# Four column tiles for the projections and the transposes of maxima in a decoder kernel on one core

## The chip, the cores and the metric

The kernel runs on one core of one Trainium2 chip. The metric is the device time of one launch in microseconds. TensorE (PE) multiplies, VectorE (DVE) and ScalarE (ACT) work on vectors, GpSimdE (POOL) helps them, SyncE (SP) issues the transfers. Each engine runs its own list of instructions in order, and they wait for each other by semaphores.

## The reference

32 sequences of 256 tokens with 256 features go through one decoder layer:

```python
x = x + attn(layernorm(x))            # 16 heads of 16, rotary positions, 256 keys
x = x + xattn(layernorm(x), ctx)      # 16 heads of 16, 77 keys
x = x + ffn(layernorm(x))
# ffn: 6 nodes, each an attention with 8 heads of 32 over earlier nodes
for c in range(6):
    nsrc = min(c + 1, 5); s = c - nsrc
    q = ew[c, 0] * (nodes[c - 1] @ We[eq] + be[eq])
    k = ew[c, 1] * (nodes[s] @ We[ek] + be[ek])
    v = ew[c, 2] * (nodes[s + nsrc // 2] @ We[ev] + be[ev])
    nodes[c] = act_w[c] * mha(q, k, v, Wq[c], Wk[c], Wv[c], Wo[c]) + q
out = layernorm(nodes[5])             # with gain and shift
```

All inputs and outputs are float32.

## The kernel before

A preamble multiplies the edge weights of the nodes with the heads' weights, so that each node needs one projection each for q, k and v, and puts all weights into SBUF. Then a loop runs 16 turns. A turn takes two sequences, slot 0 and slot 1, through eight stages: 0 is self attention, 1 cross attention, 2 to 7 the nodes. The two slots stand at different stages, so that one has work for PE while the other waits.

The work is cut into 838 pieces a turn. The text ORDER lists them, written out by hand or by a planner, and each engine runs its own pieces in that order. A word is a kind, the slot, the stage and, for some, a group of heads and a part. "@5" gives the PSUM bank (S and ST take four banks from it), and a "+" marks a piece that belongs to the next pair of sequences and is run once ahead of the loop. The last turn leaves those out.

PE's pieces are:
- TR transposes the normed tokens. Q and QB, K, V make the projections, QR and KR rotate q and k for the positions with a 128x128 matrix.
- S and SB make scores with the queries on the partitions, from which VectorE takes row maxima (MX, L879). Both factors are split into a high and a low fp32r part. These matmuls have 32 rows, one group of heads each, and four of them stand side by side in four row tiles.
- GpSimdE splits the negated maxima into two parts (NM, L695 and L698), MT transposes them (L1028), ScalarE copies them to SBUF (MR, L780).
- ST makes the scores again with the keys on the partitions, SX adds the negated maxima to them by a matmul with a selector, and ScalarE takes exp from there (EX, L789).
- PV multiplies the exponentials with ones (the sums) and with the values. Each of these matmuls writes 32 partitions, and four of them stand side by side in four column tiles.
- After RC and NR have divided by the sums, OA and OB make the output of a stage: XA adds it to the residual stream, or NE keeps it as the next node.

LOADX and LOADC load tokens and contexts, STORE writes a result, all from SP's queue. LNS, LNP, LNN norm.

Before the change Q, QB, K, V, QR, KR, OA and OB use all 128 columns of the array, for V of the cross stage 77. They go through the helper matmul, so that all of them have line L909, as have S, SB, ST, SX and PV; in the trace they are told apart by the tiles that they read. MT uses PE's transpose, 128x128, two for a piece.

Of the kernel before, what the change touches and what calls it, by code (L numbers as in the profile page):

```python
# [139 lines left out]
NM0.1.0 PV1.0.1 NM0.1.1 MT0.1.0@5 ST1.0.3@0 SX1.0.3 RC1.0.0 MR0.1.0 PV1.0.2@7 MT0.1.1@5 EX1.0.3.0 EX1.0.3.1  # L140
ST0.1.0@0 SX0.1.0 EX0.1.0.0 MR0.1.1 PV1.0.3 EX0.1.0.1 ST0.1.1@0 SX0.1.1 NR1.0.0 PV0.1.0@4 OB1.0.0@6 RC1.0.1
NR1.0.1 EX0.1.1.0 EX0.1.1.1 OB1.0.1 ST0.1.2@0 SX0.1.2 EX0.1.2.0 EX0.1.2.1 V1.1@7 VE1.1 PV0.1.1 RC0.1.0 XA1.0
LNS1.1 LNP1.1 LNN1.1 +LOADX0 +LNS0.0 PV0.1.2@5 ST0.1.3@0 SX0.1.3 EX0.1.3.0 EX0.1.3.1 NR0.1.0 +LNP0.0 +LOADC0
TR1.1@6 +K0.1@7 TRE1.1 PV0.1.3 Q1.1@1 QB1.1 RC0.1.1 NR0.1.1 QH1.1.0 QH1.1.1 QL1.1.1 QL1.1.0 +KI0.1 OB0.1.0@4
OB0.1.1 XA0.1 S1.1.0@0 SB1.1.0 MX1.1.0.0 MX1.1.0.1 S1.1.1@4 SB1.1.1 MX1.1.1.0 S1.1.2@0 SB1.1.2 MX1.1.1.1 NM1.1.1
NM1.1.0 MX1.1.2.0 MX1.1.2.1 S1.1.3@4 SB1.1.3 MX1.1.3.0 MT1.1.0@1 MR1.1.0 ST1.1.0@0 SX1.1.0 MX1.1.3.1 NM1.1.2
NM1.1.3 MT1.1.1@6 EX1.1.0.1 MR1.1.1 LNS0.2 LNP0.2 XB1.1 LNN0.2 ST1.1.1@4 SX1.1.1 EX1.1.0.0 PV1.1.0@1 TR0.2@2
EX1.1.1.0 EX1.1.1.1 ST1.1.2@4 SX1.1.2 TRE0.2 Q0.2@0 QB0.2 EX1.1.2.0 EX1.1.2.1 PV1.1.1 QH0.2.0 QH0.2.1 QL0.2.0
+LNN0.0 ST1.1.3@4 SX1.1.3 RC1.1.0 NR1.1.0 QL0.2.1 K0.2@3 PV1.1.2@2 EX1.1.3.1 EX1.1.3.0 PV1.1.3 +KH0.1 KH0.2
KL0.2 RC1.1.1 S0.2.0@4 SB0.2.0 +LOADC1 +KL0.1 +K1.1@3 +KI1.1 NR1.1.1 OB1.1.0@0 OB1.1.1 V0.2@2 K0.3@3 KH0.3  # L150
MX0.2.0.1 XA1.1 LNS1.2 LNP1.2 MX0.2.0.0 LNN1.2 S0.2.1@4 TR1.2@0 TRE1.2 NM0.2.0 MT0.2.0@1 SB0.2.1 KL0.3 K1.2@3
MR0.2.0 KH1.2 VE0.2 Q1.2@1 QB1.2 QH1.2.0 QH1.2.1 MX0.2.1.1 MX0.2.1.0 NM0.2.1 QL1.2.1 KL1.2 QL1.2.0 ST0.2.0@4
SX0.2.0 EX0.2.0.0 EX0.2.0.1 K1.3@2 KH1.3 KL1.3 MT0.2.1@0 MR0.2.1 S1.2.0@4 SB1.2.0 MX1.2.0.1 MX1.2.0.0 NM1.2.0
PV0.2.0@1 RC0.2.0 V1.2@2 VE1.2 ST0.2.1@4 SX0.2.1 EX0.2.1.0 EX0.2.1.1 NR0.2.0 K0.4@1 KH0.4 MT1.2.0@2 MR1.2.0
S1.2.1@4 SB1.2.1 MX1.2.1.1 MX1.2.1.0 PV0.2.1@3 RC0.2.1 OA0.2@0 ST1.2.0@4 SX1.2.0 EX1.2.0.1 EX1.2.0.0 KL0.4
NM1.2.1 MT1.2.1@1 MR1.2.1 OB0.2.0 NR0.2.1 OB0.2.1 NE0.2.0 NE0.2.1 ST1.2.1@4 SX1.2.1 EX1.2.1.1 EX1.2.1.0 Q0.3@1
QB0.3 PV1.2.0@0 QH0.3.0 QH0.3.1 QL0.3.0 QL0.3.1 S0.3.0@4 SB0.3.0 MX0.3.0.1 MX0.3.0.0 NM0.3.0 RC1.2.0 NR1.2.0
PV1.2.1@1 OA1.2@3 S0.3.1@4 SB0.3.1 OB1.2.0 MT0.3.0@2 K1.4@0 RC1.2.1 NR1.2.1 MX0.3.1.0 OB1.2.1 MX0.3.1.1
ST0.3.0@4 MR0.3.0 SX0.3.0 NE1.2.0 +KH1.1 Q1.3@1 NE1.2.1 QB1.3 V1.3@2 KH1.4 KL1.4 NM0.3.1 EX0.3.0.1 EX0.3.0.0
MT0.3.1@6 QH1.3.0 QH1.3.1 QL1.3.1 QL1.3.0 V0.3@3 MR0.3.1 S1.3.0@4 SB1.3.0 VE0.3 VE1.3 PV0.3.0@2 MX1.3.0.1  # L160
MX1.3.0.0 ST0.3.1@4 SX0.3.1 RC0.3.0 NR0.3.0 OA0.3@3 NM1.3.0 MT1.3.0@1 EX0.3.1.0 EX0.3.1.1 S1.3.1@4 SB1.3.1
MX1.3.1.0 MX1.3.1.1 PV0.3.1@0 MR1.3.0 RC0.3.1 OB0.3.0 NM1.3.1 MT1.3.1@2 MR1.3.1 ST1.3.0@4 SX1.3.0 EX1.3.0.0
EX1.3.0.1 NR0.3.1 OB0.3.1 K0.5@2 NE0.3.0 NE0.3.1 ST1.3.1@4 SX1.3.1 EX1.3.1.0 EX1.3.1.1 KH0.5 Q0.4@3 QB0.4
PV1.3.0@0 QH0.4.0 QH0.4.1 KL0.5 QL0.4.0 RC1.3.0 PV1.3.1@7 OA1.3@2 NR1.3.0 OB1.3.0 RC1.3.1 NR1.3.1 OB1.3.1
S0.4.0@4 NE1.3.0 SB0.4.0 QL0.4.1 MX0.4.0.0 MX0.4.0.1 NM0.4.0 Q1.4@0 K1.5@1 S0.4.1@4 SB0.4.1 MX0.4.1.0 MX0.4.1.1
NM0.4.1 NE1.3.1 V1.4@3 QB1.4 MT0.4.0@2 VE1.4 QH1.4.0 MR0.4.0 QH1.4.1 ST0.4.0@4 SX0.4.0 EX0.4.0.0 EX0.4.0.1
V0.4@2 MT0.4.1@3 QL1.4.0 QL1.4.1 S1.4.0@4 SB1.4.0 MX1.4.0.1 MX1.4.0.0 VE0.4 KH1.5 NM1.4.0 KL1.5 PV0.4.0@2
ST0.4.1@4 MR0.4.1 RC0.4.0 SX0.4.1 EX0.4.1.1 EX0.4.1.0 MT1.4.0@3 K0.6@0 NR0.4.0 S1.4.1@4 SB1.4.1 MX1.4.1.0
MX1.4.1.1 PV0.4.1@1 RC0.4.1 OA0.4@2 NM1.4.1 MT1.4.1@4 OB0.4.0 MR1.4.0 MR1.4.1 ST1.4.0@4 SX1.4.0 EX1.4.0.0
# [25 lines left out]
OB1.7.0 +NM0.0.2 NR1.7.1 OB1.7.1 +NM0.0.3 +MT0.0.1@5 FA1 +LNS1.0 LNS1.7 LNP1.7 +LNP1.0 +LNN1.0 LNN1.7 +EX0.0.0.0
+EX0.0.0.1 +ST0.0.1@0 +SX0.0.1 +MR0.0.1 +PV0.0.0@5 +EX0.0.1.1 +EX0.0.1.0 +ST0.0.2@0 +SX0.0.2 +EX0.0.2.0
+EX0.0.2.1 FG1 FX1 +PV0.0.1 +TR1.0@7 +RC0.0.0 +NR0.0.0 +ST0.0.3@0 +SX0.0.3 +TRE1.0 +PV0.0.2@6 STORE1 +EX0.0.3.1
+EX0.0.3.0 +PV0.0.3 +RC0.0.1 +Q1.0@2 +QB1.0 +OB0.0.0@7 +NR0.0.1 +QI1.0 +QC1.0 +XB1.0 +OB0.0.1 +QR1.0@6 +XA0.0
# [1025 lines left out]
```

How the kernel before makes its waits and increments, by code:

```python
            @block.gpsimd  # L465
            def _(pool):
                pool.memset(ident[:, :], 0.0).then_inc(consts, 1)
                pool.wait_ge(consts, 1)
                pool.affine_select(out=ident[:, :], in_=ident[:, :], compare_op=ALU.not_equal, fill=1.0,
                                   base=0, pattern=[[-1, P]], channel_multiplier=1).then_inc(consts, 1)
# [1 line left out]
            @block.tensor  # L472
            def _(pe):
                pe.wait_ge(first_loaded, 16 * len(first_copies))
                for n, (c, i) in enumerate(FUSED):
                    if i == 0:
                        pe.wait_ge(node_loaded[c], 16 * len(node_copies[c]))
                    if n >= 7:
                        pe.wait_ge(fused_kept, n - 6)
                    e = EDGES[c][EDGE_OF[i]]
                    for m in range(KC):
                        for k in range(KC):
# [6 lines left out]
                        for k in range(KC):  # L489
                            last = nc.tensor.matmul(psum[:, 7, col:col + 1],
                                                    w_head[:, i, c, k, o * P:(o + 1) * P],
                                                    be_c[:, e, k:k + 1], start=(k == 0), stop=(k == KC - 1))
                last.then_inc(bias_ready, 1)
                pe.wait_ge(bias_kept, 1)
                pe.wait_ge(scaled, 2 * NODES * KC)
                pe.wait_ge(fused_kept, len(FUSED))
```

## Time and profile before

| | |
|---|---|
| median of 3 runs | 5377.47 us (5376.7 to 5379.54) |
| profiled execution, its own time | 5370.64 us |
| its span, first to last instruction | 5368.8 us |
| matmul instructions | 63,708 |
| PE busy | 5045.7 us, 94% |
| DVE busy | 2790.9 us, 52% |
| ACT busy | 2493.8 us, 46% |
| mean granted TensorE clock | 0.95 |

Busy time of an engine is the time in which at least one of its instructions was in flight. The share is an average over stages with different limits, and overlapping matmuls make a busy PE look full. The granted clock is the share of 2.4 GHz that TensorE was given.

### The profile page before, as it was taken

What the parts mean: (1) busy time and instruction counts of PE and PEld (TensorE: products, weight loads), DVE (VectorE), ACT (ScalarE), POOL (GpSimd) and SP (SyncE); (2) the same over time, 40 slices, a digit from 0 to 9 for tenths busy, and PEclk for the clock granted to TensorE, in tenths of its full rate; (3) what the DMA queues carried; (4) which work ended last, traced back from release to release, by engine and by line L of the source; (5) the groups of instructions that cost most, each with busy time, mean ns of one, the idle gap of its engine ahead of it and who ended that gap; (6) DMA issues with size and microseconds to landing.
All of it is one profiled execution on the core that took longest, in us unless ns stands there. A gap on an engine that the chain in (4) does not pass through costs nothing.

```text
span 5368.8 us, 154142 instructions
## 1 busy us (share of the span) xinstructions
PE 5045.7 (94%) x63708; PEld 3726.1 (69%) x63708; DVE 2790.9 (52%) x5034; ACT 2493.8 (46%) x4737; POOL 638.7 (12%) x1734
## 2 busy tenths in 40 slices
PE   7998999989899898999989999899998989989898
PEld 6676766767677676776767667676676767767676
DVE  3545554454645545555454554545545454554544
ACT  1444544545455454444444445454454545545444
POOL 0102010020100201011020110201002010020100
PEclk8898998989999899998999989899898999989999
DMA  3000000000000000000000000000000000000000
GB/s 118 5 2 11 2 11 2 2 11 2 11 2 2 11 2 11 2 4 9 2 11 2 8 5 2 11 2 11 3 2 11 2 11 3 2 11 2 8 2 6
DMA packets 42877, 44.84 MB, mean 8 GB/s; under 512 B 11552, under 2 KB 41888, under 8 KB 42144
## 3 DMA queue, kind: packets, MB, share of 16 engines
q1 hardware_dynamic: 34192, 26.55, 1.6%
q8 instruction: 546, 8.95, 0.7%
q10 hardware_dynamic: 7952, 7.81, 0.4%
q14 instruction: 187, 1.53, 0.1%
HBM read 25.96 MB, written 8.39 MB: 6 GB/s over the span
## 4 chain that ended last, share of the span: by engine, by line
PE 50%; issue 38%; POOL 4%; DVE 3%; ACT 2%; POOLq 0%; ACTq 0%; DVEq 0%
PE banks L909 48%; DVE row_max L879 2%; ACT probs L789 2%; PE banks L1028 1%; POOL neg_max L695 1%; POOL neg_max L698 1%; POOL x_tok L680 1%; POOL inv_std L674 1%; PE banks L958 0%; ACT n_tok L723 0%; POOL var_eps L671 0%; POOLq L694 0%; DVE context_t L893 0%; ACT context_t L801 0%; POOLq L697 0%
## 5 line engine op out<-in xcount | busy, mean ns | idle before, releaser
L879 DVE TENSOR_REDUCE row_max<-banks 128x4 f32<-128x1024 f32 (+1 forms) x1280 | 1316.7, 1070 | 703.2 <-PE banks L909 698.4
L789 ACT ACTIVATE probs<-banks 128x1024 f32<-128x1024 f32 (+1 forms) x1280 | 1133.2, 935 | 528.5 <-PE banks L909 528.5
L909 PE MATMUL banks<-k_parts,q_parts 32*128 32x256 f32 x12288 | 534.7, 307 | 137.6 <-DVE row_max L879 54.4
L909 PE MATMUL banks<-node_t,w_n 128*128 128x256 f32 x2560 | 637.3, 391 | 0.0
L909 PEld LDWEIGHTS banks<-k_parts,q_parts 32*128 32x128 f32 x12288 | 433.7, 197 | 291.1 <-issue 215.5
L864 DVE SCALAR_TENSOR_TENSOR q_parts<-banks,b_n,q_parts 128x256 fp32r<-128x256 f32 x384 | 177.7, 480 | 811.6 <-ACT q_parts L753 811.6
L799 ACT ACTIVATE context_t<-banks 128x256 f32<-128x256 f32 x512 | 196.3, 383 | 793.0 <-PE banks L909 792.3
L909 PE MATMUL banks<-q_parts,k_parts 32*128 32x256 f32 x12288 | 521.8, 301 | 40.2 <-DVE row_max L879 33.7
L909 PEld LDWEIGHTS banks<-q_parts,k_parts 32*128 32x128 f32 x12288 | 420.3, 192 | 199.4 <-issue 112.0
L909 PEld LDWEIGHTS banks<-node_t,w_n 128*128 128x128 f32 x2560 | 460.2, 189 | 106.2 <-issue 26.3
L695 POOL TENSOR_TENSOR neg_max<-row_max,zeros 128x8 fp32r<-128x8 f32 x640 | 135.1, 211 | 3302.6 <-DVE row_max L879 3299.4
L909 PE MATMUL banks<-h_t,w_n 128*128 128x256 f32 x1792 | 452.3, 398 | 1.7
L909 PE MATMUL banks<-probs,ones 128*32 128x256 f32 x6144 | 414.6, 388 | 28.3 <-DVE row_max L879 19.2
L780 ACT ACTIVATE max_rows<-banks 128x256 fp32r<-128x256 f32 x512 | 193.5, 381 | 493.1 <-PE banks L1028 491.8
L909 PE MATMUL banks<-probs,v_full 128*32 128x256 f32 x6144 | 407.9, 383 | 0.0
L909 PEld LDWEIGHTS banks<-h_t,w_n 128*128 128x128 f32 x1792 | 342.0, 198 | 73.7 <-issue 16.0
L909 PE MATMUL banks<-w_n,node_t 128*128 128x256 f32 x1536 | 375.8, 388 | 0.0
L890 DVE TENSOR_TENSOR probs<-banks,context_t 128x256 f32<-128x256 f32 x448 | 189.0, 422 | 272.8 <-ACT context_t L801 270.5
L909 PEld LDWEIGHTS banks<-w_n,node_t 128*128 128x128 f32 x1536 | 281.0, 190 | 64.8 <-issue 17.5
L909 PE MATMUL banks<-context_t,w_n 128*128 128x256 f32 x1280 | 321.3, 386 | 0.0
L909 PEld LDWEIGHTS banks<-probs,v_full 128*32 128x32 f32 x6144 | 203.6, 111 | 133.8 <-issue 6.1
L909 PEld LDWEIGHTS banks<-probs,ones 128*32 128x32 f32 x6144 | 167.3, 109 | 170.2 <-issue 34.1
(126 smaller groups left out, 6237.6 us busy)
## 6 DMA issues: line engine op xcount, KB each, us to landing
x_next<-in_x SPq DMA_DIRECT2D x32, 256.0 KB, 2.6
out_y<-x_tok SPq DMA_DIRECT2D x32, 256.0 KB, 2.1
w_head<-in_wf SPq DMA_DIRECT2D x11, 256.0 KB, 11.2
...
```

Of the source, the lines that this page charges most:

```text
L674: done(pool.tensor_tensor(inv_std[s][:, n, :], var_eps[s][:, n, :], minus_half[:, :], ALU.pow), "inverse_std", a)
L680: done(pool.tensor_tensor(x_tok[s][:, :, :], (x_next if j == SELF else x_tok[s])[:, :, :], row_out[:, j:j + 1, :].to_broadcast([P, QT, D]) ...
L695: done(pool.tensor_tensor(parts[:, :, :, 2 * i], negated, zeros[:, :, :], ALU.add), "max_split", (a, "high"))
L698: done(pool.tensor_tensor(parts[:, :, :, 2 * i + 1], negated, parts[:, :, :, 2 * i].bitcast(F32), ALU.subtract), "max_split", (a, "low"))
L780: done(act.activation(max_rows[s][:, a[3], :], bank_of(("MT", s, j, a[3]))[:, 0:T], ACT.Copy), "max_rows_kept", a)
L789: done(act.activation(probs[s][0:rows, g % 2, 2 * p:2 * p + 2, 0:kt, :] .rearrange("p c k t -> p c (k t)"), psum[0:rows, b0:b0 + 2, 0:kt * T],
L799: done(act.activation(ctx_t_sb[s][:, a[3], :], bank[:, T:2 * T], ACT.Ln), "log_taken", a)
L864: done(dve.scalar_tensor_tensor(q_parts[s][:, 1, d, :], bank_of(("Q", s, j))[:, d * T:(d + 1) * T], proj_bias("Q", j, d), q_parts[s][:, 0, ...
L879: done(dve.reduce_max(row_max[s][:, g, 2 * p:2 * p + 2, :].rearrange("p c q -> p (c q)"), psum[:, b0:b0 + 2, :].rearrange("p c (q t) -> p ...
L890: done(dve.tensor_tensor(product, bank[:, T:2 * T], inverse, ALU.mult), "newton_in", (a, "product"))
L909: return nc.tensor.matmul(bank_ap, lhs, rhs, start=start, stop=stop, **kw)
L1028: last = nc.tensor.transpose(bank_of(a)[:, q * P:(q + 1) * P], neg_max[s][:, u, q, :].bitcast(F32), ident[:, :])
```

## The change

The matmuls of Q, QB, K, V, QR, KR, OA and OB and the transposes of MT are cut into up to four matmuls of 32 columns each, which write 32 partitions of the bank each. In place of the transpose MT has an ordinary float32 matmul with the identity. TR stays a transpose of full width. S, SB, ST, SX and PV are as before. All other engines have the same pieces, in another order: ORDER is written anew, with the same 838 pieces, the same ones ahead of the loop and other banks.

```diff
+        def matmul_by_columns(out_ap, lhs, rhs, start, stop):
+
+            rows = lhs.shape[-1]
+            for r in range(0, rows, ROWS):
+                last = nc.tensor.matmul(out_ap[r:min(r + ROWS, rows), :], lhs[:, r:min(r + ROWS, rows)], rhs,
+                                        start=start, stop=stop, skip_group_check=True)
+            return last
...
                 for d in range(KC):
-                    last = matmul(bank_of(a)[:, d * T:(d + 1) * T], w[:, c, d * P:(d + 1) * P],
-                                  node_input(s, j, "q")[:, c, :], c == 0 and d == 0, c == KC - 1,
-                                  skip_group_check=True)
+                    last = matmul_by_columns(bank_of(a)[:, d * T:(d + 1) * T], w[:, c, d * P:(d + 1) * P],
+                                             node_input(s, j, "q")[:, c, :], c == 0 and d == 0, c == KC - 1)
...
-                        last = matmul(bank_of(a)[:, d * T:d * T + width], w[:, c, d * P:(d + 1) * P],
-                                      src[:, c, 0:width], c == 0, c == KC - 1)
+                        last = matmul_by_columns(bank_of(a)[:, d * T:d * T + width], w[:, c, d * P:(d + 1) * P],
+                                                 src[:, c, 0:width], c == 0, c == KC - 1)
...
-                done(matmul(bank_of(a), rot[:, :], rope_in[s][:, :, :].rearrange("p k t -> p (k t)"), True, True),
-                     "proj_ready", a)
+                done(matmul_by_columns(bank_of(a), rot[:, :], rope_in[s][:, :, :].rearrange("p k t -> p (k t)"),
+                                       True, True), "proj_ready", a)
...
-                    last = nc.tensor.transpose(bank_of(a)[:, q * P:(q + 1) * P],
-                                               neg_max[s][:, u, q, :].bitcast(F32), ident[:, :])
+                    last = matmul_by_columns(bank_of(a)[:, q * P:(q + 1) * P], neg_max[s][:, u, q, :].bitcast(F32),
+                                             ident[:, :], True, True)
```

V, OA and OB are changed in the same way. The first line of the order, before and after:

```diff
-KL1.0 VE1.0 QH0.1.0 QH0.1.1 QL0.1.0 QL0.1.1 S1.0.0@0 SB1.0.0 MX1.0.0.1 S1.0.1@4 SB1.0.1 MX1.0.1.0 MX1.0.0.0
...
+VE1.0 +LOADX0 QH0.1.0 KL1.0 QH0.1.1 S1.0.0@0 SB1.0.0 QL0.1.1 QL0.1.0 MX1.0.0.1 MX1.0.0.0 S1.0.1@4 SB1.0.1
```

## Rows read from the trace of the kernel before

**Rows 1.** The page: span, busy time by engine, chain by engine
```profile
span 5368.8 us, 154142 instructions
...
PE 5045.7 (94%) x63708; PEld 3726.1 (69%) x63708; DVE 2790.9 (52%) x5034; ACT 2493.8 (46%) x4737; POOL 638.7 (12%) x1734
...
PE 50%; issue 38%; POOL 4%; DVE 3%; ACT 2%; POOLq 0%; ACTq 0%; DVEq 0%
```

**Rows 2.** Longest pieces of the chain: start us, us, what
```profile
276.46 21.66 PE banks L909 x225
...
5201.05 21.65 PE banks L909 x223
```

**Rows 3.** Windows over one turn, 1424 to 1752.6 us, their sum
```profile
core 0: us, PE busy (x) PEld busy (x) DVE busy (x) ACT busy (x) POOL busy (x), PEclk, DMA share, GB/s
...
sum 327.60, PE 309.82 PEld 227.97 DVE 172.67 ACT 155.41 POOL 39.88; mean PE 22.13 PEld 16.28 DVE 12.33 ACT 11.10 POOL 2.85
```

**Rows 4.** Windows: two stretches of low clock, and inside the node stages
```profile
1460.90:1481.40 20.50, 14.84 (x243) 13.44 (x236) 13.20 (x18) 2.47 (x4) 3.12 (x16) 0.50 0.01 2
...
1512.10:1522.30 10.20, 9.73 (x74) 5.70 (x66) 2.11 (x6) 4.20 (x8) 2.12 (x3) 0.50 0.01 2
1540.00:1740.00 200.00, 197.00 (x2440) 146.70 (x2443) 98.75 (x160) 102.16 (x194) 12.17 (x47) 1.00 0.01 2
```

**Rows 5.** PE's groups by shape: names, shapes, count | busy us, mean ns
```profile
L1028 PE MATMUL banks<-ident,neg_max 128*128 128x128 f32 x1024 | 217.3, 299 | 8.7 <-ACT n_tok L723 4.0 <-POOL neg_max L698 2.9
...
L909 PE MATMUL banks<-h_t,w_qkv 128*128 128x256 f32 x512 | 124.2, 385 | 0.0
```

**Rows 6.** Timeline of PE, 1000 to 1010 us: start us, us, what
```profile
1000.18 1.99 PE L909 MATMUL banks<-node_t,w_n 128*128 128x256 f32 x8
1002.01 0.38 PE L1028 MATMUL banks<-ident,neg_max 128*128 128x128 f32 x2
1002.38 0.98 PE L909 MATMUL banks<-k_parts,q_parts 32*128 32x256 f32 x24
1003.30 1.07 PE L909 MATMUL banks<-probs,ones 128*32 128x256 f32 x16
1004.19 1.05 PE L909 MATMUL banks<-probs,v_full 128*32 128x256 f32 x16
1005.16 1.99 PE L909 MATMUL banks<-node_t,w_n 128*128 128x256 f32 x8
1007.09 0.99 PE L909 MATMUL banks<-q_parts,k_parts 32*128 32x256 f32 x24
1007.90 0.40 PE L909 MATMUL banks<-max_rows,select 32*128 32x256 f32 x8
1008.24 1.13 PE L909 MATMUL banks<-context_t,w_n 128*128 128x256 f32 x4
1009.20 0.38 PE L1028 MATMUL banks<-ident,neg_max 128*128 128x128 f32 x2
1009.42 1.03 PE L909 MATMUL banks<-context_t,w_n 128*128 128x256 f32 x4
```

**Rows 7.** Timeline of PE at 1004.7 us
```profile
1004.40 0.61 PE L909 MATMUL banks<-probs,v_full 128*32 128x256 f32 x8
```

**Rows 8.** Timeline of PE in the cross stage
```profile
1500.26 0.29 PE L909 MATMUL banks<-max_rows,select 32*77 32x256 f32 x4
...
1501.23 1.01 PE L909 MATMUL banks<-c_t,w_x 128*128 128x77 f32 x8
1502.17 0.64 PE L909 MATMUL banks<-probs,half_ones 77*32 77x256 f32 x8
```

**Rows 9.** PE's waits: us in total, times, longest us
```profile
PE banks L909 <- DVE row_max L879: 147.9, 151, 2.9
PE banks L909 <- ACT probs L789: 42.3, 112, 2.1
...
PE banks L909 <- DMA c_t<-in_ctx_t: 5.9, 1, 5.9
```

**Rows 10.** Timeline of PE ahead of the second stretch of low clock
```profile
1507.01 3.54 PE L909 MATMUL banks<-kx_parts,q_parts 32*128 32x78 f32 x96
```

More of the change, by code:

```diff
@@ L140 @@
[L140 to L169, printed above, removed]
@@ L195 @@
[L195 to L198, printed above, removed]
-+K1.0@5 +LNS0.1 +QS1.0 +LNP0.1 +KI1.0 +KC1.0 +LNN0.1 +QH1.0.1 +QL1.0.1 +V0.1@1 +KR1.0@3 +TR0.1@5 +VE0.1 +KS1.0
@@ new lines @@
+KL1.4 QL1.3.0 QL1.3.1 S1.3.0@4 SB1.3.0 MX1.3.0.1 MX1.3.0.0 VE0.3 V1.3@0 VE1.3 PV0.3.0@3 ST0.3.1@4 MR0.3.1
+SX0.3.1 +KH1.1 K0.5@2 NM1.3.0 MT1.3.0@1 EX0.3.1.1 EX0.3.1.0 MR1.3.0 RC0.3.0 S1.3.1@4 SB1.3.1 MX1.3.1.0 PV0.3.1@0
+OA0.3@1 MX1.3.1.1 ST1.3.0@4 SX1.3.0 RC0.3.1 EX1.3.0.0 EX1.3.0.1 NR0.3.0 OB0.3.0 NM1.3.1 NR0.3.1 OB0.3.1
+MT1.3.1@3 MR1.3.1 ST1.3.1@4 SX1.3.1 PV1.3.0@3 OA1.3@0 EX1.3.1.1 EX1.3.1.0 NE0.3.0 PV1.3.1@7 RC1.3.0 NR1.3.0
+KH0.5 KL0.5 Q0.4@3 OB1.3.0 NE0.3.1 QB0.4 RC1.3.1 NR1.3.1 OB1.3.1 QH0.4.0 QH0.4.1 QL0.4.0 NE1.3.0 NE1.3.1
@@ new lines @@
+OA0.7@1 MT1.7.0@0 +KR0.0@3 MR1.7.0 +KC0.0 +KS0.0 ST1.7.0@4 +KH0.0 +KL0.0 SX1.7.0 EX1.7.0.1 EX1.7.0.0 OB0.7.0
+OB0.7.1 FA0 LNS0.7 V1.7@2 VE1.7 +S0.0.0@4 +SB0.0.0 +MX0.0.0.1 NM1.7.1 +MX0.0.0.0 PV1.7.0@2 LNP0.7 RC1.7.0
+NR1.7.0 MT1.7.1@3 ST1.7.1@4 MR1.7.1 SX1.7.1 +S0.0.1@0 +SB0.0.1 +NM0.0.0 LNN0.7 +MX0.0.1.0 +MX0.0.1.1 FG0
+EX1.7.1.0 EX1.7.1.1 +S0.0.2@4 +SB0.0.2 +MX0.0.2.0 +MX0.0.2.1 +S0.0.3@0 +SB0.0.3 +MX0.0.3.0 +NM0.0.1 FX0
++MX0.0.3.1 +NM0.0.2 PV1.7.1@5 RC1.7.1 +NM0.0.3 NR1.7.1 OA1.7@4 +MT0.0.0@6 +MR0.0.0 STORE0 +ST0.0.0@0 +SX0.0.0
@@ L201 @@
++KH1.0 +V1.0@0 +Q0.1@6 +QB0.1 +XB0.1
 """
@@ L999, in tensor_step @@
                     for c in range(KC):
-                        last = matmul(bank_of(a)[0:n, q * D:(q + 1) * D], src[:, c, t0:t0 + n], w[:, c, :],
-                                      c == 0, c == KC - 1)
+                        last = matmul_by_columns(bank_of(a)[0:n, q * D:(q + 1) * D], src[:, c, t0:t0 + n],
+                                                 w[:, c, :], c == 0, c == KC - 1)
                 done(last, "proj_ready", a)
@@ L1083, in tensor_step @@
                         lhs, rhs = (w[:, c, cut], src[:, c, :]) if FFN0 <= j < LAST else (src[:, c, cut], w[:, c, :])
-                        last = matmul(bank_of(a)[:, half * T:(half + 1) * T], lhs, rhs,
-                                      half == c == 0 and (k == "OA" or j < FFN0), k == "OB" and c == KC - 1,
-                                      skip_group_check=True)
+                        last = matmul_by_columns(bank_of(a)[:, half * T:(half + 1) * T], lhs, rhs,
+                                                 half == c == 0 and (k == "OA" or j < FFN0),
+                                                 k == "OB" and c == KC - 1)
                 if k == "OA" or a[3] == KC - 1:
```

84 lines of the change are left out of this document (54 added, 30 removed).

## Prediction

> **What bounds the kernel now.** I read the page first. TensorE (PE) has work in flight for 94% of the span and the chain that ended last is half PE; VectorE and ScalarE are about half busy [rows 1]. So what counts is how much time PE needs for its stream of pieces and where it stands still. A turn of the loop (two sequences) is the distance between two equal places of the chain, fifteen turns apart: (5201.05 - 276.46) / 15 = 328.3 us [rows 2]. The windows over one turn show PE busy in 309.8 of 327.6 us, idle in about 18 [rows 3]. In the middle of the turn, where the six node stages run, it is busy in 197.0 of 200 us at full clock [rows 4]: there a saved or added PE nanosecond counts in full. In the self and cross attention part stand two stretches at a granted clock of 0.50, which is 1.2 GHz, the lower level: 20.5 us in which PE is 14.8 us busy and mostly waits for the maxima, and 10.2 us in which it is busy all but 0.5 us [rows 4].
>
> Busy time can't tell what a piece costs, for matmuls overlap. Start-to-start times can. The groups tell how many instructions a call makes: the self stage's h_t,w_qkv has 8 calls per slot and turn, 8 x 2 x 16 = 256, and the trace has 512; MT has 32 pieces of 2 transposes, 32 x 2 x 16 = 1024, and the trace has 1024 [rows 5]. So an ordinary f32 matmul is two instructions, a transpose is one.
>
> The timeline of a stretch without waits then gives the prices [rows 6]. Call F the work on all 128 columns, C the four column tiles of 32 (PV), R the four row tiles of 32 (S, SB, ST, SX).
> - F, 256 columns: 1.99 us for 8 instructions and 1.13 for 4 differ by 0.215 each; I write 0.216.
> - C, 256 columns: four sets of four last 1.05 [rows 6] and two sets 0.61 [rows 7], so 0.22 a set, the same 0.216. The four tiles go side by side and a set costs what one full-width instruction costs. **Column tiles as such give nothing and cost nothing.**
> - R: two sets 0.40 [rows 6], one set 0.29 [rows 8], about 0.115; with the 8 sets below I use 0.118.
> - A transpose of 128 columns: two take 1009.42 - 1009.20 = 0.22, 0.109 each.
> - Changing the kind. F entered from R and left to a transpose, itself F: 1002.01 - 1000.18 = 1.83, against 8 x 0.216 = 1.73: entering F costs 0.104. F entered from C and left to R: 1.93, so leaving F costs about 0.09 (1.93 - 1.73 - 0.104; I use 0.093). C: 4 sets take 0.89 from entry (0.864 without), entering costs 0.025; the next 4 up to an F take 0.97, leaving C costs 0.11 (I use 0.113). R: 8 sets from F to F take 1.15 against 0.94, 0.09 to enter and 0.10 to leave to F. R before a PV: 0.92 against 6 x 0.118 = 0.71, so 0.21 for entering and leaving, 0.12 to leave. A transpose entered from another kind pays 0.055 instead of 0.104 (estimate: half, for half the columns).
>
> **The change, part by part.** The same 838 pieces run in both orders, so nothing is added or removed but instructions.
>
> *Switches.* I counted neighbours among the PE pieces of each order, the turn closed to a ring. Before: F to R 52, R to F 44, R to C 23, C to F 19, C to R 15, F to C 11; 17 of the 63 entries into F are transposes. Leaving: 63 x 0.093 + 34 x 0.113 + 44 x 0.10 + 23 x 0.12 = 16.9 us. Entering: 67 x 0.09 + 46 x 0.104 + 17 x 0.055 + 34 x 0.024 = 12.6. Together 29.4 us a turn. After, only TR is F: C to R 66, R to C 64, and 12 with a TR. Leaving 69 x 0.113 + 64 x 0.12 + 3 x 0.10 + 6 x 0.093 = 16.3; entering 67 x 0.09 + 69 x 0.024 + 6 x 0.055 = 8.0. Together 24.4. **The switches give back 5.1 us a turn.** The number of changes falls from 164 to 142, and most of the gain is the cheaper entry into C. Bounds: of the 0.21 for R before a PV the entry may be 0.105 or 0.075, so leaving R to C costs 0.107 or 0.136; the one gives 5.6, the other 4.4.
>
> *MT.* 32 pieces a turn have 2 transposes each, one instruction of 0.109. As ordinary f32 matmuls each becomes two instructions on each of four tiles, two sets of 128 moving columns. A set of C costs what an F instruction costs at 256 columns, so I take 0.109 a set too: 64 x (2 x 0.109 - 0.109) = **7.0 us a turn lost**. Upper bound: the set can't step faster than R's 0.118: 64 x (0.236 - 0.109) = 8.1. In the node stages (22 of the 32) nothing covers this, and only the filled queue hides the later MR copy; elsewhere MT stands in the chain maxima, MT, MR, SX, EX and delays it by the same 0.22 us a piece.
>
> *K of the cross stage* has 77 moving columns. Eight instructions up to the next PV take 0.94, without the exit 0.106 each [rows 8], more than 77/256 of 0.216 = 0.065. Here the 128-wide weight load may be what it waits for, and 32-wide loads would free it. Between 0 and 16 x (0.106 - 0.065) = 0.66 us a turn; I take 0.6.
>
> *Q, QB, K, V, QR, KR, OA, OB* keep their time by the equal 0.216: nought, 0.02 later at a piece's end since the tiles start some ns apart. Matmuls grow from 63,708 to about 99,900 (9,600 full-width ones times four, the 128 of cross V times three, MT's 1,024 times eight); PV runs at that density already [rows 7], so nought.
>
> *The order.* LOADX0 moves from mid-turn to its head, K of slot 0's cross stage and the context loads move a few pieces; every DMA is issued as often as before, and in PE's waits a DMA stands once with 5.9 us, where VectorE's row_max has 147.9 in 151 waits and ScalarE's probs 42.3 [rows 9]. Behind the loads on SP's queue stand only the stores. I can't price the new order's waits from this trace. It can't take away more than the 18 us of idle, nor much of the DVE-bound part; I take nought and keep about 4 us of either sign.
>
> *Sum:* -5.1 + 7.0 - 0.6 = +1.3 us a turn, 16 turns +21 us. Made against the profiled execution (5370.6, of which 5368.8 is span) that is 5392; the median of the runs stands 6.8 higher, so **5398 us**. The bounds of the terms give +0.7 (5.6, 7.0, 0.66) to +3.7 (4.4, 8.1, 0) a turn: +11 to +59, 5389 to 5437. About 0.2% (11 us) is what a measurement of this kernel can tell from no change.
>
> **Rivals.**
> 1. *The order wins back a low-clock stretch or its worth in waits: faster.* The second stretch at 0.50 costs about half of its 9.7 busy us, 4.9 us a turn. It begins soon after thin R work with 78 columns [rows 10]. If its pieces now follow dense work and it stays at full clock, the turn is 1.3 - 4.9 = -3.6: 5398 - 78 = 5320. It decides as soon as 2 us of idle a turn go. For it: with F and C one kind, the order is free to fill holes. Against: the holes are mostly waits for VectorE's maxima [rows 9], whose work is unchanged.
> The Trainium skill ("TensorE: Matmul & The Clock Gate", Part 4) says that transpose mode doesn't count as busy for the clock, which would favour this rival; but the node stages hold two thirds of MT and run at 1.00 throughout [rows 4], so the trace gives it little weight.
> 2. *MT costs nothing more: faster.* If the identity matmul took one instruction per tile, the 7.0 go: -5.7 a turn, 5377 - 91 = 5286. Against: every other f32 matmul has two [rows 5].
> 3. *It evens out: same.* 1.3 us less of waits a turn.
> 4. *A further wait or low stretch: slower by more.* One like the second adds 4.9: 5398 + 78 = 5476. For it: the later MT pushes MR, SX and EX, and ACT holds them in a strict order.
> 5. *An identity matmul costs four times the transpose.* If so, MT loses 64 x 3 x 0.109 = 20.9 us a turn instead of 7.0: 5398 + 222 = 5620. Against: two instructions of 0.109 each follow from rows 5 and 6.
> The Trainium skill, same page, "Terms", calls transpose mode 4x faster for FP32. Rows 5 and 6 put it at twice.
>
> **How the numbers follow.** Forecast (terms as bounded, order neutral) 0.43; rival 1 with smaller gains of the order 0.25; rival 2 0.07; rival 3 0.12, rival 4 0.11, rival 5 0.02. Faster: rivals 1 and 2, and a little of 3's spread, 0.34. Same: rival 3 and the lower edge of the forecast, 0.17. Slower 0.49. The range leaves out rival 2, rival 5 and the full size of rivals 1 and 4's outer halves: 5318 to 5450. The forecast's own range is 5389 to 5437.
>
> **What would show it.** A set of the new projections steps by 0.216 us; its entry after scores costs 0.02, not 0.10; PV runs into a projection without a break. MT shows 8,192 instructions in place of 1,024, 0.44 us a piece in place of 0.22. No full-width group but ident,n_tok stays in the loop. The node part of the turn is longer by about 1 us, the rest likewise, and two stretches at 0.50 remain. It is wrong if MT has 4,096, if the sets of 128 columns step by much more than 0.118, if the longer MT shows up as PE waits for max_rows, or if the number or length of low-clock stretches changes.

## Result and the profile after

The changed kernel takes 5304.8 us (median of 4 runs, 5302.8 to 5306.6) against 5377.1: 0.9865 of the time, 95% interval 0.9848 to 0.9882. That is 72 us faster. The prediction said 21 us slower and gave a range from 5318, so it missed in sign and range. (The kernel before stood at 5377.1 us here and at 5374.1 to 5375.3 in the experiments below, so that a difference of an experiment to the changed kernel is unsure by some 2 us.)

The page of the profile after:

```profile
span 5300.9 us, 226544 instructions
...
PE 5031.6 (95%) x99932; PEld 3265.7 (62%) x99932; DVE 2805.3 (53%) x5034; ACT 2497.0 (47%) x4737; POOL 632.7 (12%) x1734
...
q8 instruction: 817, 13.39, 1.0%
...
PE 74%; issue 14%; DVE 4%; ACT 3%; POOL 2%; POOLq 0%; ACTq 0%; DVEq 0%
```

PE is busy 14 us less than before (5031.6 against 5045.7 [rows 1]), the span is 68 us shorter. There are 99,932 matmuls in place of 63,708, and 817 transfers of instructions, 16 KB each, where the page before has 546:

```profile
q8 instruction: 546, 8.95, 0.7%
```

PE's groups, for the two whose counts the prediction rested on:

```profile
L915 PE MATMUL banks<-ident,neg_max 128*32 128x128 f32 x8192 | 343.5, 290 | 2.8 <-POOL neg_max L698 1.9 <-DVE row_max L879 0.6
...
L915 PE MATMUL banks<-h_t,w_qkv 128*32 128x256 f32 x2048 | 122.8, 380 | 0.0
```

Against [rows 5] the counts are four times 512, and eight times 1024: the identity matmul of MT is two instructions on each of four tiles. The timeline of PE, first in a node stage, then at a K of the cross stage (start us, us, what), shows the prices again:

```profile
1200.68 1.93 PE L915 MATMUL banks<-h_t,w_n 128*32 128x256 f32 x32
1202.43 0.62 PE L915 MATMUL banks<-ident,neg_max 128*32 128x128 f32 x16
1202.98 0.98 PE L909 MATMUL banks<-k_parts,q_parts 32*128 32x256 f32 x24
1203.90 1.07 PE L909 MATMUL banks<-probs,ones 128*32 128x256 f32 x16
1204.79 1.05 PE L909 MATMUL banks<-probs,v_full 128*32 128x256 f32 x16
1205.65 1.91 PE L915 MATMUL banks<-h_t,w_n 128*32 128x256 f32 x32
1207.49 0.98 PE L909 MATMUL banks<-q_parts,k_parts 32*128 32x256 f32 x24
1208.30 0.41 PE L909 MATMUL banks<-max_rows,select 32*128 32x256 f32 x8
1208.64 0.65 PE L915 MATMUL banks<-ident,neg_max 128*32 128x128 f32 x16
1209.10 1.91 PE L915 MATMUL banks<-context_t,w_n 128*32 128x256 f32 x32
```

```profile
1153.27 0.72 PE L915 MATMUL banks<-c_t,w_x 128*32 128x77 f32 x32
1153.92 0.66 PE L966 MATMUL banks<-ident,n_tok 128*128 128x128 f32 x4
```

From scores into a projection and out of it to MT, itself in column tiles now: 1202.43 - 1200.68 = 1.75 for eight sets, 8 x 0.216 + 0.02. With full-width work it was 1.83 [rows 6]. PV runs into a projection without a break (1205.65 - 1204.79 = 0.86, 4 x 0.216). MT between R and C: 1209.10 - 1208.64 = 0.46, four sets of 0.109 and the entry. So each price that these rows can show was met, MT's doubling too. The time came from elsewhere.

One turn, cut into four stretches at events that all kernels have: the start of the gain multiplication of slot 0's output, the ends of XA0.0, XA1.0 and XA1.1, and the next gain multiplication. PE's loop jumps back in the second stretch. First the kernel before, then the changed one; each row has the stretch, its length, busy us and count for PE, PE's weight loads, DVE, ACT and POOL, the granted clock, DMA share and GB/s.

```profile
core 0: us, PE busy (x) PEld busy (x) DVE busy (x) ACT busy (x) POOL busy (x), PEclk, DMA share, GB/s
1420.60:1449.40 28.80, 25.60 (x386) 17.81 (x382) 16.51 (x33) 13.01 (x20) 11.14 (x19) 1.00 0.09 29
1449.40:1497.60 48.20, 39.48 (x566) 29.80 (x565) 24.47 (x40) 18.01 (x34) 8.17 (x21) 0.79 0.04 10
1497.60:1532.40 34.80, 33.17 (x388) 22.79 (x386) 19.95 (x52) 15.34 (x38) 5.53 (x15) 0.85 0.02 4
1532.40:1748.60 216.20, 212.17 (x2629) 158.32 (x2631) 111.78 (x186) 109.38 (x207) 14.97 (x54) 1.00 0.01 2
```

```profile
1397.40:1425.20 27.80, 25.64 (x523) 16.33 (x520) 18.34 (x33) 13.17 (x21) 11.93 (x17) 1.00 0.13 41
1425.20:1472.60 47.40, 39.64 (x738) 27.75 (x733) 25.17 (x44) 17.71 (x33) 7.99 (x22) 0.82 0.02 5
1472.60:1506.60 34.00, 32.22 (x608) 19.80 (x606) 17.97 (x48) 15.53 (x38) 4.59 (x13) 0.85 0.02 5
1506.60:1720.80 214.20, 212.16 (x4388) 136.10 (x4380) 111.81 (x187) 109.49 (x207) 14.99 (x57) 1.00 0.01 3
```

All four stretches are shorter, by 1.0, 0.8, 0.8 and 2.0 us in these turns. The first differs from turn to turn, though: in the kernel before it takes 28.9 us in seven of the first fourteen turns and 30.3 to 30.5 in the other seven, which hold 3.4 us at the lower clock. Such a turn, to set against the first row above, in which they begin 0.6 us after 1.28 us of idle time of PE that e8 is about:

```profile
1090.10:1120.60 30.50, 27.31 (x391) 18.58 (x384) 16.56 (x33) 13.07 (x20) 11.26 (x19) 0.94 0.08 27
```

In the changed kernel it is 27.8 us in eight turns and 29.1 to 29.3 in six.

In the last stretch, the node stages, PE is busy for 212.2 us in both: tiles and MT about cancel, and what shrank is PE's idle time, from 4.0 to 2.0 us. PE's waits in the whole run say the same (us in total, times, longest):

```profile
PE banks L909 <- DVE row_max L879: 93.0, 169, 1.7
PE banks L909 <- ACT probs L789: 51.1, 127, 2.1
PE banks L909 <- DVE q_parts L864: 30.3, 10, 3.2
```

Waits for VectorE's row maxima fell from 147.9 us to 93.0 [rows 9].

### The profile page after: what moved, and what is told of

It is laid out like the page before. It is cut to its first block, busy times and chain, and to the rows that moved or that the text cites. A ratio compares the mean times of both kernels' runs of the same rounds, so it can differ in the third digit from the quotient of the medians.

```text
span 5300.9 us, 226544 instructions
## 1 busy us (share of the span) xinstructions
PE 5031.6 (95%) x99932; PEld 3265.7 (62%) x99932; DVE 2805.3 (53%) x5034; ACT 2497.0 (47%) x4737; POOL 632.7 (12%) x1734
## 4 chain that ended last, share of the span: by engine, by line
PE 74%; issue 14%; DVE 4%; ACT 3%; POOL 2%; POOLq 0%; ACTq 0%; DVEq 0%
PE banks L915 38%; PE banks L909 35%; DVE row_max L879 3%; ACT probs L789 2%; PE banks L966 1%; POOL neg_max L695 0%; POOL inv_std L674 0%; POOL neg_max L698 0%; POOL x_tok L680 0%; DVE rope_s L848 0%; ACT k_parts L747 0%; ACT n_tok L723 0%; DVE rope_s L844 0%; DVE q_parts L851 0%; DVE context_t L893 0%
## 5 line engine op out<-in xcount | busy, mean ns | idle before, releaser
L915 PE MATMUL banks<-node_t,w_n 128*32 128x256 f32 x10240 | 632.2, 380 | 0.0
L915 PEld LDWEIGHTS banks<-node_t,w_n 128*32 128x32 f32 x10240 | 316.8, 110 | 203.4 <-issue 2.5
L915 PE MATMUL banks<-h_t,w_n 128*32 128x256 f32 x7168 | 442.0, 390 | 0.0
L915 PE MATMUL banks<-w_n,node_t 128*32 128x256 f32 x6144 | 369.7, 381 | 3.3 <-ACT n_tok L723 3.3
L915 PE MATMUL banks<-ident,neg_max 128*32 128x128 f32 x8192 | 343.5, 290 | 2.8 <-POOL neg_max L698 1.9
L915 PEld LDWEIGHTS banks<-h_t,w_n 128*32 128x32 f32 x7168 | 229.6, 113 | 159.9 <-issue 24.6
L915 PE MATMUL banks<-context_t,w_n 128*32 128x256 f32 x5120 | 318.8, 380 | 0.0
L915 PEld LDWEIGHTS banks<-ident,neg_max 128*32 128x32 f32 x8192 | 239.6, 115 | 90.6 <-issue 13.9
```

The source lines that it names most:

```text
L915: last = nc.tensor.matmul(out_ap[r:min(r + ROWS, rows), :], lhs[:, r:min(r + ROWS, rows)], rhs, start=start, stop=stop, skip_group_check=True)
```

## Experiments

All times are medians; the ratio is against runs of the kernel before on the same chip, with its 95% interval. A turn's length is worked out from the starts of slot 0's gain multiplication.

| run | order | wide or columns | MT | PE turns a pass | us | ratio (interval) |
|---|---|---|---|---|---|---|
| e1 | old | columns | columns | 1 | 5391.4 | 1.0029 (1.0019 to 1.0040) |
| e2 | new | wide | transpose | 1 | 5358.4 | 0.9966 (0.9954 to 0.9979) |
| e3 | new | columns | transpose | 1 | 5306.5 | 0.9866 (0.9851 to 0.9881) |
| e4 | new | columns | mixed | 1 | 5312.3 | 0.9880 (0.9865 to 0.9895) |
| e5 | new | columns | columns | 3 | 5292.2 | 0.9846 (0.9834 to 0.9859) |
| e6 | new | columns | transpose | 3 | 5271.7 | 0.9808 (0.9795 to 0.9821) |
| e7 | new, S twice | columns | columns | 1 | 5346.0 | 0.9951 (0.9939 to 0.9963) |
| e8 | old, one swap | wide | transpose | 1 | 5355.2 | 0.9962 (0.9949 to 0.9975) |
| e9 | old | wide | transpose | 3 | 5367.9 | 0.9986 (0.9977 to 0.9995) |
| e10 | old | columns | columns | 3 | 5383.6 | 1.0014 (1.0005 to 1.0023) |
| e11 | new | wide | transpose | 3 | 5344.9 | 0.9947 (0.9934 to 0.9961) |
| e12 | new | columns | mixed | 3 | 5265.3 | 0.9798 (0.9785 to 0.9811) |
| e13 | new, swap undone | columns | columns | 1 | 5331.5 | 0.9918 (0.9905 to 0.9932) |
| e14 | old, one swap | columns | mixed | 3 | 5317.7 | 0.9901 (0.9886 to 0.9916) |

### Which half of the change: e1 and e2

e1 is the changed code with the old text of ORDER, e2 the code of before with the new text.

> The order of before with all the column tiles of the change. Theory O (the new order took PE's waits and low-clock time away, whatever the tiles): only the terms of the forecast are left, switches -5.9, MT +7.0, K of the cross stage -0.6 us a turn, so +0.5 us a turn, about 5385 us, within 0.3% of before, and waits plus low-clock loss as before, some 37 us a turn. Theory T (the column tiles themselves shorten waits, for results come earlier or the clock is held): most of the gain is here already, 5300 to 5330.

Measured 5391.4, 16 us above the kernel before. Theory T is gone: the tiles alone gain nothing. The sum is near the forecast's +21 us, but that is partly luck, as the table below shows. (The switches of the old order, counted again with the forecast's prices, are 29.4 us a turn wide and 24.4 in tiles, so 5.1 and not the 5.9 that was expected here.)

> The new order with the full-width projections and the transposes of before. Theory O: the waits stay as short as in the changed kernel; against it the switches cost 8.2 us a turn more, MT 7.0 less, K of the cross stage 0.6 more: +1.8 us a turn, about 5334 us, faster than before by 0.8%. Theory T: no gain without the tiles, and the order's 13 more switches of work into full width make it 5377 to 5415.

Measured 5358.4: 17 us faster than before, so the order is worth something without the tiles, but 24 us less than theory O said. With tiles the order is worth 5391.4 - 5304.8 = 87 us, without them 17. The switches explain part of that: by the prices the new order pays 2.3 us a turn, 37 us, more for them with wide work (177 changes of kind against 164, 8 of the 13 more into a full-width piece), and nothing more with tiles (142 changes in either order). Counted so, the wide work costs the new order 7.3 us a turn of switches more than tiles, not the 8.2 of the expectation.

e1's turn in the same four stretches, 30.5, 50.1, 33.9 and 216.3 us:

```profile
1425.50:1456.00 30.50, 27.30 (x521) 17.03 (x519) 16.48 (x33) 13.03 (x20) 11.17 (x19) 0.94 0.09 29
1456.00:1506.10 50.10, 39.82 (x742) 28.20 (x738) 24.50 (x39) 18.04 (x34) 8.15 (x21) 0.83 0.04 10
1506.10:1540.00 33.90, 31.84 (x602) 19.68 (x598) 19.94 (x54) 15.42 (x38) 5.52 (x15) 0.85 0.02 5
1540.00:1756.30 216.30, 212.37 (x4388) 136.17 (x4379) 111.80 (x186) 110.01 (x207) 15.04 (x55) 1.00 0.01 3
```

Against before the node stages cost the same (216.3 and 216.2), where the forecast had about 1 us more. The second stretch costs 1.9 us more. That had no term in the forecast, and it stands where PE's loop jumps back. (The traces of e1 and e13 are of their slowest executions, 5405.3 and 5339.7 us, that of e9 is of its fastest, 5360.7.)

The traces tell where a turn's time goes. The table has means over the first fourteen turns of each: the turn, the time in which PE has nothing in flight, and PE's busy time at the lower clock. The last column is an estimate of PE's work, its busy time with that at the lower clock counted half, for a PV half with the next projection behind it took 1098.19 - 1096.31 = 1.88 us at the lower clock in the kernel before and 0.97 at full clock [rows 6]. It comes out alike for kernels with the same PE work (298.3, 298.4 and 298.4 for before, e8 and e9). The other runs are told of further below. The two rows of before at the lower clock:

```profile
1096.31 1.96 PE L909 MATMUL banks<-probs,v_full 128*32 128x256 f32 x16
1098.19 2.42 PE L909 MATMUL banks<-w_n,node_t 128*128 128x256 f32 x8
```


| run | turn, us | PE idle | busy at the lower clock | work |
|---|---|---|---|---|
| before | 328.6 | 17.7 | 25.2 | 298.3 |
| changed | 324.1 | 14.3 | 23.2 | 298.2 |
| e1 | 330.9 | 19.3 | 27.5 | 297.8 |
| e2 | 327.6 | 13.7 | 26.4 | 300.7 |
| e3 | 324.5 | 16.2 | 23.9 | 296.3 |
| e5 | 323.2 | 13.6 | 22.1 | 298.5 |
| e6 | 321.8 | 14.9 | 20.7 | 296.5 |
| e7 | 326.5 | 13.2 | 22.0 | 302.2 |
| e8 | 327.5 | 16.9 | 24.2 | 298.4 |
| e9 | 327.7 | 17.7 | 23.3 | 298.4 |
| e10 | 329.3 | 18.5 | 26.0 | 297.8 |
| e11 | 326.5 | 14.0 | 23.2 | 300.8 |
| e13 | 326.0 | 15.0 | 25.9 | 298.1 |

From before to changed a turn loses 4.5 us: 3.4 of idle time, 1.0 by less work at the lower clock (half of 25.2 - 23.2), 0.1 of work. The new order with wide work (e2) loses as much idle time, 4.0 us, but its work grows by 2.4, close to the 2.3 of the switches. In the old order the tiles' work is 0.5 us less, not 1.3 more; e1 is slower by idle time and the lower clock, which no term of the forecast had.

### MT as a transpose: e3 and e4

```diff
-                    last = matmul_by_columns(bank_of(a)[:, q * P:(q + 1) * P], neg_max[s][:, u, q, :].bitcast(F32),
-                                             ident[:, :], True, True)
+                    last = nc.tensor.transpose(bank_of(a)[:, q * P:(q + 1) * P],
+                                               neg_max[s][:, u, q, :].bitcast(F32), ident[:, :])
```

> The changed kernel with MT as the transpose of before, at full width; all else in column tiles. If the price of MT as an ordinary matmul is right (7.0 us a turn) and the switches into and out of full width are worth 5.1, this gives -1.8 us a turn, 5275 us. If MT is hidden behind other work, or the earlier end of a transpose is worth nothing, the switches alone decide: +5.1 us a turn, 5386.

e4 takes the transpose only where a neighbour of MT among PE's pieces is S, SB, ST, SX or TR:

```python
WIDE_MT = [a for n, a in enumerate(PE_PIECES) if a[0] == "MT"
           and {PE_PIECES[n - 1][0], PE_PIECES[(n + 1) % len(PE_PIECES)][0]} & {"S", "SB", "ST", "SX", "TR"}]
```

> As the one before, but 7 of the 32 MT pieces a turn, those with only column-tile work on both sides, stay in column tiles (0.44 us and no switch against 0.22 us and 0.29 of switches). By the prices 2.3 us a turn less than the changed kernel: 5268 us, 7 us less than with all 32 as transposes. If the prices of single switches are not what PE's time is made of, no difference between the two.

Measured 5306.5 and 5312.3: neither gain came. The price of an MT had just been seen in the timeline, so something took it up. The place is again the head of the turn. At the jump of the loop PE's next piece is S1.0.0, which waits for the key parts that VectorE writes. Kernel before, VectorE's row and PE's:

```profile
1458.16 1.41 DVE L857 SCALAR_TENSOR_TENSOR k_parts<-rope_s,own_half,k_parts 128x512 fp32r<-128x512 f32 x2 [2.09 <-ACT k_parts L747]
```

```profile
1455.50 1.89 PE L909 MATMUL banks<-h_t,w_x 128*128 128x256 f32 x8
1460.05 1.00 PE L909 MATMUL banks<-k_parts,q_parts 32*128 32x256 f32 x24 [2.65 <-ACT q_parts L753]
```

Key parts done at 1458.16 + 1.41 = 1459.57, PE starts at 1460.05, 0.48 us later. The changed kernel:

```profile
1110.46 1.41 DVE L857 SCALAR_TENSOR_TENSOR k_parts<-rope_s,own_half,k_parts 128x512 fp32r<-128x512 f32 x2 [2.08 <-ACT k_parts L747]
```

```profile
1108.53 1.93 PE L915 MATMUL banks<-h_t,w_x 128*32 128x256 f32 x32 [0.37 <-DVE rope_s L848]
1113.64 2.93 PE L909 MATMUL banks<-k_parts,q_parts 32*128 32x256 f32 x48 [3.17 <-DVE q_parts L864]
```

Done at 1111.87, start at 1113.64: 1.77 us. And e3:

```profile
1113.81 1.41 DVE L857 SCALAR_TENSOR_TENSOR k_parts<-rope_s,own_half,k_parts 128x512 fp32r<-128x512 f32 x2 [2.28 <-ACT k_parts L747]
```

```profile
1111.68 1.93 PE L915 MATMUL banks<-h_t,w_x 128*32 128x256 f32 x32 [0.36 <-DVE rope_s L848]
1117.78 0.82 PE L909 MATMUL banks<-k_parts,q_parts 32*128 32x256 f32 x17 [4.17 <-DVE q_parts L864]
1120.31 2.08 PE L909 MATMUL banks<-k_parts,q_parts 32*128 32x256 f32 x31 [1.70 <-issue]
```

Done at 1115.22, start at 1117.78, 2.56 us later, and after 17 matmuls a second gap of 1.70 us, put down to "issue": PE waited for nothing that the profile shows.

### PE's jump: e5, e6, e9

```diff
-        def turns(engine, step):
+        def turns(engine, step, unroll=1):
...
-            with engine.Fori(0, ITERS - 1) as it:
-                for a in PLAN:
-                    step(engine, it, a)
+            with engine.Fori(0, (ITERS - 1) // unroll) as it:
+                for u in range(unroll):
+                    raised.clear()
+                    for a in PLAN:
+                        step(engine, it if unroll == 1 else it * unroll + u, a)
...
-            turns(pe, tensor_step)
+            turns(pe, tensor_step, 3)
```

> The changed kernel, but PE's program alone runs three turns a pass of its loop, so that it jumps back 4 times and not 14; the other engines' loops are as they were. In the changed kernel the first matmul after PE's jump starts 1.4 to 1.8 us after the key parts that it waits for are written, in the kernel before 0.5 us. Theory F (at the jump PE waits for its instructions, and the change's longer program has laid this wait open): 10 jumps less at some 1.2 us, 12 us faster than the changed kernel, about 5293. Theory D (the delay is VectorE's or the clock's): no difference, 5305.

> Transposes for MT, column tiles for the rest, and PE's loop of three turns. With PE's loop of one turn the transposes gained nothing, where the prices said 1.8 us a turn, and in that trace PE stands still twice after the jump, before the first matmul (up to 2.4 us) and again for 1.5 to 2.3 us before the 18th. Theory F: both go at 10 of 14 jumps, some 30 us: 5275, under the changed kernel with the same loop. Theory C (the transposes' gain was lost to the granted clock, whose lower stretches are 3 us a turn longer): 5300, no better than the changed kernel with the same loop.

> The kernel before with PE's loop of three turns. Its first matmul after the jump starts 0.47 us after the key parts, as early as after no jump in the runs with three turns, so the wait for instructions lies under the wait for the key parts: 0 to 5 us faster, 5370 to 5375.

Measured 5292.2 (12.6 us less than the changed kernel, expected 12), 5271.7 (34.8 us less than e3, expected about 30) and 5367.9 (7 us less than before, a little more than expected). Nothing but PE's loop differs, so the jump is shown to cost in the changed kernel and more in e3's program. Inside e6 it can be seen turn by turn: turns without a jump take 320.6 to 320.9 us, those with one 324.2 to 324.7, about 3.8 us more; in the second stretch all four hold 20.5 us at the lower clock, where most of the others hold 13.7, and three of them 10.2 us or more of idle time, the others 7.4 to 8.3. In e5 the clock hides it in the turn's length, but the first matmul comes 1.3 to 1.6 us after the key parts in the four turns with a jump and 0.4 to 0.6 in the others. In e9 turns with a jump are no longer than the rest (327.6 and 327.8 us), so where its 7 us lie isn't shown.

That PE waits for the transfer of its own instructions there is the likely reading. The gap has no other releaser, and in the changed kernel the start of a transfer of 16 KB on queue q8 falls within 0.1 us of that first matmul in each turn (1113.64 us for both in the turn above); in e5 the two are at most 0.13 us apart in the four turns with a jump and 0.45 or more in the others. The Trainium skill ("Runtime: NRT & Kernel Launch", Instruction fetch mechanics) says that a taken branch out of the fetched window forces such a transfer before execution goes on. The trace agrees in that the late start and the transfer go together.

With fewer jumps MT's transposes are worth 5292.2 - 5271.7 = 20.5 us, where the prices say 29. By the table PE's work falls by 2.0 us a turn (e5 to e6), 32 us, so the price holds; 1.3 us of idle time a turn take part of it back, and the four jumps that are left cost e6 more than e5. With a jump a turn the same shows more: from the changed kernel to e3 the work falls by 1.9 us a turn, and 1.9 us of idle time and 0.4 by the clock take it all back. The mixed form is checked by

> MT mixed (7 pieces a turn in column tiles, 25 as transposes), PE's loop of three turns. The prices make it 0.5 us a turn less than all transposes: 5264. If the waits take that up, or if the mixed kernel has more low clock as with the loop of one turn, 5272 or more.

which gave 5265.3, 6.4 us under e6 where 8 were expected. In e3 and e4, with a jump a turn, the same edit had cost 6 us. e12 is the fastest kernel of this study, 40 us under the changed kernel and 110 under the one before.

### The granted clock: e7

```diff
-                for q in range(QT):
+                twice = k == "S" and (s, j) in ((1, SELF), (0, CROSS))
+                for q in list(range(QT)) * (1 + twice):
```

> The changed kernel, with the matmuls of S made twice for slot 1's self stage and slot 0's cross stage (8 pieces a turn, 128 more matmuls, 3.7 us at full clock), where PE waits for the row maxima of the group before. The second pass starts afresh and writes the same. If the granted clock falls there because PE does too little, the first low stretch (17 us) vanishes or shrinks: its matmuls then run at 2.4 GHz, and the turn is 2 to 6 us shorter, 5210 to 5270. If the clock stays at 0.50 all the same, the doubled matmuls cost 7 us at the lower level, of which PE's waits for the maxima hide 4 to 5: 5335 to 5360.

Measured 5346.0, 41 us slower than the changed kernel. In most turns the first stretch of low clock shrank from 13.7 or 17.1 us to 10.2 or 13.7, so more work did raise the clock, but the turn grew by 2.4 us. The doubled groups while the maxima are awaited, in e7:

```profile
1126.71 1.50 PE L909 MATMUL banks<-k_parts,q_parts 32*128 32x256 f32 x40 [0.32 <-DVE row_max L879]
...
1133.50 6.53 PE L909 MATMUL banks<-kx_parts,q_parts 32*128 32x78 f32 x120 [0.95 <-DVE row_max L879]
```

and single in the changed kernel, in a turn with the same pattern of clock:

```profile
1117.74 0.98 PE L909 MATMUL banks<-k_parts,q_parts 32*128 32x256 f32 x24 [1.18 <-DVE row_max L879]
...
1124.53 4.06 PE L909 MATMUL banks<-kx_parts,q_parts 32*128 32x78 f32 x72 [0.76 <-DVE row_max L879]
```

A self-stage group of 24 or 40 matmuls waits for the maxima either way. The cross-stage groups of 78 columns pay in full, 6.53 us for 120 in place of 4.06 for 72. By the table 4.0 us of work came in, and 1.1 of idle time and 0.6 by the clock went. Bought with double work the clock is a loss. The time lies in the second range expected, 5335 to 5360, but by neither mechanism: the clock did rise in part.

### One wait in the order: e8 and e13

e8 exchanges two neighbours in the old order:

```diff
-+MX0.0.2.1 +MX0.0.2.0
++MX0.0.2.0 +MX0.0.2.1
```

> The kernel before with two neighbours of VectorE's order exchanged: MX0.0.2.0 now comes ahead of MX0.0.2.1, as in the new order. PV1.7.1 waits for bank 4, which the former empties; the trace shows 1.28 us of PE idle there in each turn, ended by row_max. If such waits are what the new order took away, and nothing later takes this one up: 1.2 us a turn less, 5357. If VectorE's or ScalarE's later pieces set the pace there, no difference.

Measured 5355.2, 20 us faster for one exchange. The rows of before,

```profile
1423.29 0.98 PE L909 MATMUL banks<-k_parts,q_parts 32*128 32x256 f32 x24 [0.80 <-DVE row_max L879]
1425.55 1.07 PE L909 MATMUL banks<-probs,ones 128*32 128x256 f32 x16 [1.28 <-DVE row_max L879]
```

have 1.28 us of idle ahead of PV1.7.1, and those of e8 have none:

```profile
1418.39 0.98 PE L909 MATMUL banks<-k_parts,q_parts 32*128 32x256 f32 x24 [0.81 <-DVE row_max L879]
1419.53 1.07 PE L909 MATMUL banks<-probs,ones 128*32 128x256 f32 x16
```

Up to the end of XA0.0 the turn takes 28.1 to 28.4 us in each of fourteen turns, all at full clock, as in this one:

```profile
1415.70:1443.90 28.20, 25.81 (x386) 17.69 (x382) 16.40 (x33) 13.07 (x20) 11.04 (x19) 1.00 0.10 30
```

Before it was 28.9 at full clock, or 30.3 to 30.5 with 3.4 us at the lower one, 29.7 on average. So the exchange takes 1.5 us off this stretch, about 0.7 by the wait and 0.8 by the clock, which no longer falls there. Over the whole turn 1.1 is left; 0.3 is lost again in the second stretch.

> The changed kernel with MX0.0.2.1 ahead of MX0.0.2.0 again, as in the old order; PV1.7.1, now in bank 5, still waits for MX0.0.2.0. If this one place gives the changed kernel what it gave the old order (20 us), it is 5325. If in the new order another piece would have to wait there anyway, 5305.

Measured 5331.5, 27 us slower than the changed kernel. The first stretch is 28.9 us in seven turns and 31.3 to 31.6, with 6.8 us at the lower clock, in seven, where the changed kernel had 27.8 and 29.1 to 29.3. So this one place is a third of what the new order gives the changed kernel, and again the clock has a part in it: of the 1.8 us by which this stretch is longer on average, some 1.1 are the wait and the rest the lower clock.

### What the tiles are worth without the jump: e10, e11, e14

> The old order with all column tiles, PE's loop of three turns. With one turn the first matmul after the jump starts 1.8 to 2.1 us after the key parts. Theory F: 1.5 us less at 10 jumps, 5376, and against the kernel before with the same loop only the terms of the forecast are left, +0.5 to +1.3 us a turn: 8 to 21 us slower than that. If tiles cost more than these terms somewhere else, it stays at 5391.

> The new order with full-width work and transposes, PE's loop of three turns. Its first matmul comes 0.8 us after the key parts, and a second gap of 1.0 to 1.5 us stands before the 32nd matmul: 10 times up to 1.2 us, 5346. If the tiles are worth in the new order what the terms say (1.8 us a turn), it stands 29 us above the changed kernel with three turns: 5321. If it is 5346, the tiles are worth twice the terms in this order.

Measured 5383.6, 16 us above e9: inside the +8 to +21 expected, but again not by the terms, for by the table the work is 0.6 us a turn less than e9's and idle time and the clock make the difference. e10 lost less to the jump than expected (8 us less than e1, not 15). And 5344.9, 53 us above e5: in the new order the tiles are worth 53 us, where the 1.8 us a turn expected make 29 and the forecast's own prices (7.3 - 7.0 + 0.6 = 0.9 us a turn) 15. By the table the turns differ by 3.3 us, 2.3 of work, 0.5 by the lower clock and 0.4 of idle time. So most of it is work, more than the prices have, and 1.4 us of the turn lie between the ends of XA0.1 and XA1.1 (25.7 against 24.3 us, means). Why wide projections cost more there in this order was not tried.

> The old order with the one exchange of VectorE's pieces, column tiles for the projections, MT mixed (4 pieces a turn in column tiles, 28 as transposes), PE's loop of three turns. From the kernel before with three turns (5368): exchange -20, terms of tiles and MT -2.3 us a turn, -37: 5311. The same parts in the new order gave 5265; if 5311 comes out, the rest of the new order (waits in the node stages and at the head of the turn) is worth the other 46 us. If it is 5340 or more, the terms don't hold in the old order.

Measured 5317.7, 7 us above the sum of its parts. The same parts in the new order are e12's 5265.3. So the new order beyond the one exchange is worth 52 us.

## Why the prediction was wrong

- **The step that failed** is the order: "I can't price the new order's waits from this trace ... I take nought and keep about 4 us of either sign." With the tiles the order was worth 87 us, 5.4 us a turn (e1 against the changed kernel), beyond even those 4. Against the kernel before, PE's idle time fell from 17.7 to 14.3 us a turn, its waits for the row maxima from 147.9 to 93.0 us in all, and less work at the lower clock gave about 1.0 us a turn. One wait, which the trace before showed in each turn with its releaser, is 20 us in the old order and 27 in the new, with the clock that falls beside it. I read the waits' total and took them as set by VectorE's unchanged work; it was the sequence of that work that set them.
- **Rival 1** had the right direction and wrote down the right reason (with F and C one kind the order is free to fill holes), but I priced it by a stretch of low clock. Both stretches remained, on average shorter (18.5 and 10.2 us a turn before, 16.6 and 8.5 after), and a third one of 3.4 us, which the forecast didn't see, stands in seven of fourteen turns before and in six after. The waits shrank more, in the node stages alone by 2 us a turn. Of the 72 us the clock gave some 16 by the estimate of the table, the idle time some 54. Rivals 3 and 4 are out by the time; a further wait as in rival 4 did come, at the jump, but under a larger gain.
- **The switches** (-5.1 us a turn): the prices that the timeline shows were met. Their sum was tested only together with MT and K: e1 gave +16 us and e10 +16 against +21. That nearness is luck in part: the work of a turn fell by 0.5 to 0.6 us in the old order, where the terms add up to +1.3, and the rest came from idle time and the clock. Which term is too dear was not found.
- **MT** (+7.0): the count (8,192) and the 0.44 us a piece came as worked out. Rivals 2 and 5 are out by the count. Taking MT back gained 20.5 us net of 29, once the jump was rare. The upper bound rested on "the set can't step faster than R's 0.118"; the sets step by 0.109.
- **K of the cross stage**: where it runs alone, its 32 matmuls (the second timeline above) fill 1153.92 - 1153.27 = 0.65 us up to the next matmul, 0.081 for each of the eight sets with the change to full width. Without 0.11 for that they step by 0.068, so that K gives 16 x (0.106 - 0.068) = 0.61 us a turn, as the 0.6 that I took.
- **The instructions**: "PV runs at that density already, so nought" held within a stretch and was wrong at the loop's end. In the kernel before the first matmul after the jump comes 0.4 to 0.5 us after the key parts, and in e9, with a jump or without, 0.4 to 0.6. The longer program laid open 1.0 to 1.3 us a jump (12.6 us for 10 jumps fewer, 10 by the ratios), and 3.5 with the transposes (34.8), which made e3 look as if MT's price were wrong.
- **Not settled**: why the work is less than the prices say, by 1.8 us a turn in the old order and 1.4 in the new, and how the last 52 us of the order divide among its many small differences.
